# Turning the row maxima of a head group with VectorE's 32-wide transposes instead of TensorE's transpose and ScalarE's copy

## The reference

```python
xn = _layernorm(x, axis=-1)
x = x + _L0_attn_ref(xn, ...) + _L0_ffn_ref(xn, ...)
```

```python
attn = jnp.einsum('bhqd,bhkd->bhqk', q, k) * scale
attn = jax.nn.softmax(attn, axis=-1)
out = jnp.einsum('bhqk,bhkd->bhqd', attn, v)
```

## Time and profile before

| what | value |
|---|---|
| median of 3 runs | 946.4 us (944.36 to 946.92) |
| the profiled execution | 944.99 us, its span 943.2 us |
| granted TensorE clock over the span | 0.969 of full |
| PE busy | 871.3 us, 92% of the span |
| PEld busy | 605.1 us, 64% |
| DVE busy | 608.0 us, 64% |
| ACT busy | 583.3 us, 62% |
| POOL busy | 427.3 us, 45% |

### The profile page before, as it was taken

How to read it: one execution, slowest core, us unless ns; L and a number is a source line. 1 busy time by engine, 2 the same in 40 slices (tenths; PEclk the granted TensorE clock), 3 DMA queues, 4 the chain that set the end, 5 groups by cost and what they waited for, 6 DMA issues and landing times.

```text
span 943.2 us, 19555 instructions
## 1 busy us (share of the span) xinstructions
PE 871.3 (92%) x6491; PEld 605.1 (64%) x6492; DVE 608.0 (64%) x914; ACT 583.3 (62%) x941; POOL 427.3 (45%) x417
## 2 busy tenths in 40 slices
PE   5846999999999989889999999999999999999996
PEld 2436999999999976456556555555565465565462
DVE  6787844444444455676786786786777877776752
ACT  5855744444444442767767767767767866856764
POOL 2104722222222151753753764854754844744831
PEclk9965999999999999999999999999999999999997
DMA  9884555222222216554854755755755655654310
GB/s 315 315 265 149 187 151 172 72 72 68 76 67 69 65 47 171 157 154 101 203 158 118 198 159 127 198 155 130 189 163 130 192 161 130 191 141 109 76 48 23
DMA packets 91479, 133.74 MB, mean 142 GB/s; under 512 B 17512, under 2 KB 51824, under 8 KB 91024
## 3 DMA queue, kind: packets, MB, share of 16 engines
q1 hardware_dynamic: 84720, 114.95, 43.3%
q0 software_dynamic: 6480, 17.70, 7.1%
q10 hardware_dynamic: 208, 0.14, 0.0%
HBM read 76.10 MB, written 51.56 MB: 135 GB/s over the span
## 4 chain that ended last, share of the span: by engine, by line
PE 80%; DVE 11%; issue 3%; ACT 2%; DMA 2%; POOL 1%; DVEq 0%; ACTq 0%; POOLq 0%
PE bank L1463 12%; PE bank L1503 10%; PE s_pair L1412 9%; PE bank L1359 8%; PE s_pair L1341 8%; PE bank L1568 7%; PE st_pair L1491 6%; PE st_pair L1341 6%; DVE top L1934 4%; PE bank L1349 2%; PE bank L1324 2%; DMA xg<-xn_rows,token_of 1%; PE bank L1476 1%; PE bank L1517 1%; PE bank L1402 1%
## 5 line engine op out<-in xcount | busy, mean ns | idle before, releaser
L1934 DVE TENSOR_REDUCE top<-s_pair 128x2 f32<-128x1024 f32 x248 | 303.7, 1225 | 134.1 <-PE s_pair L1412 131.2
L1120 ACT ACTIVATE prob<-st_pair 128x1024 f32<-128x1024 f32 x252 | 259.1, 1028 | 116.9 <-PE st_pair L1491 109.1
L780 POOL DMA_INDIRECT xg<-xn_rows,token_of x71 | 82.7, 1165 | 207.5 <-PE bank L1324 157.3
L1463 PE MATMUL bank<-xT_b,w_sh 64*128 64x512 f32 x960 | 143.2, 404 | 0.5
L1412 PE MATMUL s_pair<-k_rows,q_rows 48*128 48x512 f32 x496 | 115.6, 459 | 12.0 <-DVE top L1934 11.8
L1503 PE MATMUL bank<-prob,v_ones 128*32 128x512 f32 x1024 | 124.8, 605 | 0.0
L1463 PEld LDWEIGHTS bank<-xT_b,w_sh 64*128 64x128 f32 x960 | 91.7, 187 | 31.1 <-issue 8.3
L1491 PE MATMUL st_pair<-q_rows,k_rows 50*128 50x512 f32 x504 | 106.2, 415 | 3.4 <-ACT prob L1120 2.6
L1359 PE MATMUL bank<-w_exp,c_hT 128*128 (+1 forms) x639 | 94.2, 292 | 0.6 <-ACT c_y L1027 0.6
L1412 PEld LDWEIGHTS s_pair<-k_rows,q_rows 48*128 48x128 f32 x496 | 47.4, 184 | 64.9 <-DVE top L1934 55.4
L1341 PE MATMUL s_pair<-w_exp,xg_T 128*128 x468 | 88.1, 338 | 0.0
(11 more groups left out here) (238 smaller groups left out, 1240.6 us busy)
## 6 DMA issues: line engine op xcount, KB each, us to landing
qk_rows<-qk_hi SPq DMA_DIRECT2D x56, 256.0 KB
q_rows<-qk_rows SPq DMA_DIRECT2D x64, 192.0 KB
k_rows<-qk_rows SPq DMA_DIRECT2D x56, 192.0 KB
expert_rows<-c_y SPq DMA_DIRECT2D x71, 128.0 KB, 1.7
qk_rows<-qk_lo SPq DMA_DIRECT2D x28, 256.0 KB
x_all<-in_L_attn_x_dram SPq DMA_DIRECT2D x8, 512.0 KB, 7.3
xn_rows<-x_n SPq DMA_DIRECT2D x8, 512.0 KB, 3.5
o_b<-in_L_attn_x_dram SPq DMA_DIRECT2D x8, 512.0 KB, 6.5
```

Of the source, the lines that this page charges most:

```text
L780: pool.indirect_dma_start(xg[s % 4][:, :], None, xn_dram, bass.IndirectOffsetOnAxis(token_of[:, s:s + 1], 0)).then_inc(c_x[s % 4], 16)
L1120: act.activation(prob[n % 3][:, 2 * jp:2 * jp + 2, :].rearrange("p j l -> p (j l)"), score_T_pair(b, g, t)[:, :], ACT.Exp, scale=HD ** -0. ...
L1463: ins = pe.matmul((g_bank, u_bank)[up][:, :], w_sh[rows, a, o:o + P], xT_of(b)[rows, c, k, :], start=(n == 0 and i == 0), stop=(n == 1 and ...
L1934: dve.tensor_reduce(top[g % 2][:, :, jp, qt], score_pair(b, g, v)[:, :].rearrange("p (i k) -> p i k", i=2), AX_X, ALU.max).then_inc(d_max, 1)
```

## The change

`turn_max` on PE and `max_rows` on ACT are gone. In their place `split_max` issues four more DVE instructions, each of which transposes 32 partitions x 32 columns of `top_parts` (the 16 columns and 16 beside them) into columns r to r + 31 of `top_T`; all four write partitions 0 to 31, and they read partitions from 0, 32, 64 and 96. `load_max` waits for them. PE's other uses of `m_bank`, which had waited for ACT's copy, now wait for what ran before it.

```diff
             def load_max(b, g):
-                wait(sp, a_mt, b * NG + g + 1)
+                wait(sp, d_mt, b * NG + g + 1)
...
-            def max_rows(b, g):
-                wait(act, b_mt, b * NG + g + 1)
-
-                wait(act, m_in[g % 2], (2 * b + g // 2) * 32)
-                act.activation(top_T[g % 2][:, :], m_bank[0:32, 0:P], ACT.Copy).then_inc(a_mt, 1)
...
-            def turn_max(b, g):
-                wait(pe, d_m, b * NG + g + 1)
...
-                pe.transpose(m_bank[0:32, 0:P], top_parts[g % 2][:, :, :, :, :].rearrange("p i a j t -> p (i a j t)").bitcast(F32),
-                             ident_f[:, :]).then_inc(b_mt, 1)
...
                 dve.tensor_tensor(dst[:, :, LO, :, :], src, dst[:, :, HI, :, :].bitcast(F32), ALU.subtract).then_inc(d_m, 1)
+                wait(dve, d_m, b * NG + g + 1)
+                wait(dve, m_in[g % 2], (2 * b + g // 2) * 32)
+                for r in range(0, P, 32):
+                    ins = dve.transpose(top_T[g % 2][:, r:r + 32], dst[r:r + 32, :, :, :, :].rearrange("p i a j t -> p (i a j t)").bitcast(F32))
+                ins.then_inc(d_mt, 1)
```

More of the change, by code:

```diff
@@ L261, in build_program @@
         top_parts = [sb(f"top_parts{i}", [P, 2, 2, 2, TPB], F32R, late) for i in range(2)]
-        top_T = [sb(f"top_T{i}", [32, P], F32R, late) for i in range(2)]
+        top_T = [sb(f"top_T{i}", [32, P], F32, late) for i in range(2)]
         xT_bs = [xT_b, xT_1]
@@ L343, in build_program @@
         inv_in = sem("inv_in")
[L345 to L351, removed]
+        b_r, b_v, b_qk, b_s, b_st, b_pv, b_gu, b_ha, b_res, b_dn, b_po = (
+            sem(f"b_{n}") for n in ("r", "v", "qk", "s", "st", "pv", "gu", "ha", "res", "dn", "po"))
+        a_r, a_v, a_qk, a_exp, a_th, a_uh, a_hh, a_ot, a_ao, a_res = (
+            sem(f"a_{n}") for n in ("r", "v", "qk", "exp", "th", "uh", "hh", "ot", "ao", "res"))
+        d_r, d_qk, d_max, d_mh, d_m, d_mt, d_ga, d_hb, d_inv, d_res, d_dn, d_po = (
+            sem(f"d_{n}") for n in ("r", "qk", "max", "mh", "m", "mt", "ga", "hb", "inv", "res", "dn", "po"))
         b_to, b_bo, d_to, a_bo, d_bo = (sem(n) for n in ("b_to", "b_bo", "d_to", "a_bo", "d_bo"))
@@ L655, in load_max @@
             def load_max(b, g):
-                wait(sp, a_mt, b * NG + g + 1)
+                wait(sp, d_mt, b * NG + g + 1)
                 for par in range(2):
                     sp.dma_start(q_rows[g][64 * par + 48:64 * par + 50, :, :].rearrange("a j (t q) -> a j t q", q=P).bitcast(F32),
-                                 top_T[g % 2][16 * par:16 * par + 16, :].bitcast(F32)).then_inc(m_in[g % 2], 16)
+                                 top_T[g % 2][16 * par:16 * par + 16, :]).then_inc(m_in[g % 2], 16)
             def move_sums(b, g):
@@ L1152, in slot @@
                         up_half(c, q)
-                    if t == 5 and there(nb):
-                        max_rows(nb, ng)
                     if now:
@@ L1181, in slot @@
                         last_o_high(0)
-            max_rows(0, 0)
             low_rank_high(1)
@@ L1396, in project @@
                 elif n == 1:
-                    wait(pe, a_mt, (b - 1) * NG + 2)
+                    wait(pe, d_qk, b * 4 + 1)
                 elif n == 2:
@@ L1400, in project @@
                 else:
-                    wait(pe, a_mt, (b - 1) * NG + 3)
+                    wait(pe, d_qk, b * 4 + 3)
                 pe.matmul(m_bank[:, :], w_rows[:, which, half * P:(half + 1) * P], r_rows[b % 2][:, which, :], start=True, stop=True).then_inc(b_qk, 1)
@@ L1510, in low_rank @@
                 wait(pe, xT_in, 16) if b == 1 else wait(pe, p_xl, b - 1)
-                if b <= 2:
-                    wait(pe, a_mt, 1 if b == 1 else 4)
+                if b == 1:
+                    pe.wait_ge(c_hed, NS - 1)
+                elif b == 2:
+                    wait(pe, d_qk, 8)
                 else:
@@ L1524, in project_values @@
                     wait(pe, r_in, b * 48 + 48)
-                    wait(pe, a_mt, b * NG + 1)
-                    if b == 0:
-                        pe.wait_ge(d_r, 2)
+                    wait(pe, d_r, b + 2) if there(b + 1) else wait(pe, d_po, (b - 1) * 2)
                 elif there(b + 1):
@@ L1530, in project_values @@
                 else:
-                    wait(pe, a_mt, b * NG + 2)
+                    wait(pe, a_v, b * 2 + 1)
                 for t in range(TPB):
@@ L1581, in project_o @@
                 elif h == 0:
-                    wait(pe, d_qk, (b + 2) * 4 + 4) if there(b + 2) else wait(pe, a_mt, (b + 1) * NG + 3)
+                    wait(pe, d_qk, (b + 2) * 4 + 4) if there(b + 2) else wait(pe, a_v, (b + 1) * 2 + 2)
                 else:
-                    wait(pe, a_mt, (b + 1) * NG + 4)
+                    wait(pe, d_po, b * 2 + 1)
                 for n in range(2):
@@ L1670, in slot @@
                         values(b, g, 1)
-                    if t == 4 and there(nb):
-                        turn_max(nb, ng)
                     if (g, t) == (1, 0) and now:
@@ L1693, in _ @@
             some_tiles(NS // RUN * RUN, last=True)
-            turn_max(0, 0)
             score(0, 1, 0)
@@ L1937, in split_max @@
                 wait(dve, d_max, b * 32 + g * 8 + 8)
-                wait(dve, b_mt, b * NG + g - 1)
+                wait(dve, d_mt, b * NG + g - 1)
                 dst = top_parts[g % 2]
```

## The result

The change takes 959.74 us in the median of four runs (956.57 to 962.18), the kernel before 946.66 in four runs beside it (944.36 to 948.04): a ratio of 1.014, 95% interval 1.0108 to 1.0172. The profiled executions are 956.57 and 944.99 us, 11.6 apart, so the profiles show nearly all of what the medians (13.1) do.

What follows compares the result with a forecast made beforehand. PE's queue plus its waits, chiefly for DVE's maximum, was taken to bound the kernel; delays beyond each group's room, net of PE's gains, sum to 14.3 us: 959.3 from the profiled 944.99, said as 960, range 949 to 967.

Steps and rivals of the forecast that it cites:

- The hold: DVE's four transposes, reading different groups of 32 partitions, and the step 3 operation do not overlap: 0.24 us a step.
- d: Delay of DVE at maximum 0, from the transposes ahead of the step 3 operation: 1.08 us.
- The wait behind the split, 0.21: On DVE, the first transpose starts 0.21 us after the subtract, the split's second half.
- The rooms, 0.62 in twelve and 0.91 in the g = 2 groups: Delay of maximum 0 that score 1 tolerates; beyond it, 0.46 us lost in each of twelve groups, 0.17 in six.
- The four in which PE waited already: Groups where score 1 already followed maximum 0 by 0.05 or 0.06 us: 1.08 us lost each, 4.3 together.
- the five between: Groups with rooms of 0.17, 0.32, 0.45, 0.50 and 0.50 us before score 1: 3.5 us lost together.
- The two near the end: Groups with room 0.68 us, where part of the delay falls in DVE's idle time: 0 lost.
- `add_down` late, 0.6 us: In six g = 2 slots, PE's down matmuls wait for a later `add_down`: 0.1 us each, 0.6 together.
- Full overlap: Rival: transposes overlap like ordinary small DVE operations, 0.11 us a step; 945 to 947 us, chance 0.12.
- faster rival: Rival: transposes some 0.05 us apart on DVE keep PE's 0.22; sum about -5, 940 to 941 us, chance 0.06.
- dear price: Rival: each DVE transpose as slow as a reciprocal, 0.38 us a step held; 975 us, chance 0.06.
- queue behind POOL: Rival: DVE transposes stopped by running POOL operations in four or five groups; 5 us more, 965 us, chance 0.16.

Runs made afterwards that it cites:

- added-alone run: Kernel before, keeping PE's transpose and ACT's copy, with DVE also making the four transposes into a tile nothing reads: 958.06 us, ratio 1.0156.
- first experiment: The change with all four DVE transposes reading partitions 0 to 31, instruction count unchanged: 944.15 us, ratio 0.9999 to the kernel before.

## Why the prediction was right

960 was forecast and 959.74 measured, inside the range. The mechanism held, but an agreement of 0.3 us is luck: the medians' difference has an interval of 10 to 16 us, and terms of the sum that were off balanced each other. The steps:

- **What bounds the kernel.** Held. PE has less to do and the kernel is slower; the wait that grew is the loop through `s_pair` (the earlier trace rows and its answer). The added-alone run shows the queue's gain turned into waiting.
- **The hold.** The step on which all hung was taken from a PSUM row for inputs in SBUF. The first experiment shows it: 0.213 from one transpose to the next against 0.107, 1.4% against nothing. Its size was somewhat off: 0.24 a step was forecast (0.21 and 0.03 behind it); the transposes last 0.199 and the next starts 0.014 after the end (0.84 us for four), so d is 1.00, not 1.08. The other bound, 0.19, was nearer. The Trainium skill states this hold in "VectorE: DVE Perf Modes", section "Two Vector instructions with no wait between them"; the runs agree for inputs in SBUF, 1.014 against 0.9999.
- **What is held.** Not everything behind them: in the five places without a step 3 operation, maximum 0, which reads PSUM alone, starts 0.98 us after the subtract, 0.06 before the last transpose ends; with the four behind the gate, maximum 1 starts at 512.26 and they end at 511.49 + 0.84 = 512.33. The step 3 operation, which also reads SBUF, waits for the end (512.40, next at 512.44). So the forecast that it is held was right, and it is not so for every follower.
- **The wait behind the split, 0.21.** Measured 0.20 (511.36 to 511.56). Held.
- **The rooms, 0.62 in twelve and 0.91 in the g = 2 groups.** 0.61 and 0.91 by the offsets. With d = 1.00 a typical group loses 0.38 where 0.46 was forecast, a g = 2 group 0.09 where it was 0.17. The same sum with d = 1.00 is 12 x 0.38 + 6 x 0.09 - 0.2 + 4 x 1.00 + (5.00 - 1.94) - 0.4 + 0.2 = 11.8 us against 11.6 between the profiles.
- **The sum, kind by kind.** Even this comes out in part by balance. By the offsets the twelve groups lost 6.6 us, not 4.6: eight lost 0.38 or 0.39, four lost 0.5 to 1.35, and in each of these a cast or subtract was stopped by POOL. The four in which PE waited already lost 2.5, not 4.0 (in one of them a cast was stopped before and is not now), the five between 3.5, not 3.1. The two near the end, put at 0, kept PE's gain: -0.22 each.
- **`add_down` late, 0.6 us.** The down matmuls do start later behind score 1 in a g = 2 slot, 0.66 us instead of 0.56 (568.00 - 567.34, below), but the next maximum is later by only 0.03. Mis-sized: 0.2 in all.

```profile
566.07 1.22 DVE L1906 TENSOR_REDUCE top<-s_pair 128x2 f32<-128x1024 f32 x1
567.20 0.75 DVE L1947 TENSOR_TENSOR o_b<-bank,o_b 128x256 f32<-128x256 f32 x2
567.34 0.50 PE L1403 MATMUL s_pair<-k_rows,q_rows 48*128 48x512 f32 x2 [0.24 <-DVE top L1906]
...
568.00 1.45 PE L1543 MATMUL bank<-w_sh,h_T 64*128 64x256 f32 x20
```

- **Score 1 at 0.05 after maximum 0.** In 27 of 31 groups (0.04 to 0.06). It was said for g = 0, 1 and 3; it holds in g = 2 as well, where 0.17 of loss was counted, so it could have been said of g = 2 too.
- **The wait of about 30 us.** 29.0.
- **The delays add up, none is made up.** Held: all maxima but 0 and 1 change the offset by 0.9 us together.
- **The rivals.** Full overlap is what the first experiment builds, and it costs nothing, as it was worked out (945 to 947 beside 946.4; measured 944.15 beside 944.5). The sum of the faster rival is about -4 us by its own terms, not -5; nothing hangs on it. The dear price is excluded by 199 ns. The queue behind POOL is excluded for the transposes: 28 of the 128 ran while a POOL `TENSOR_TENSOR` ran, and the longest of all took 203 ns. The cast and the subtract do get stopped, 12 of 64 times (6.9 us) after 11 of 64 (6.1 us) before, in other groups. That is much of the scatter in single groups, and it happens to balance here. The slot of the earlier trace rows has a cast stopped in place of a subtract:

```profile
473.23 1.29 POOL L818 TENSOR_TENSOR ao<-ao,o_sum 128x512 f32<-128x512 f32 x1
473.52 1.04 DVE L1913 CAST top_parts<-top 128x16 fp32r<-128x16 f32 x1
```

## What to carry to other kernels

Before work is moved off a full engine, look at what the receiving engine does in the loop that both meet in: measure its room ahead of the next thing that is waited for (here 0.62 us), and price the addition against that room, not against its idle share (DVE was a third idle, and the kernel lost 1.4%). A gain on one engine and a delay on the other in front of the same wait do not add; the later one alone counts. Several small DVE operations that read different groups of 32 partitions can cost more than as many on one group (0.84 us against 0.48 for four). And time saved in front is lost again if the result needs longer on its way (one transpose instead of four saved DVE 0.6 us a group, and its DMAs cost the kernel 9%).

## What the runs showed of the hardware

- Four 32x32 transposes on DVE that read the same 32 partitions start 0.135, 0.093 and 0.093 us apart (199 ns for the first, 157 for the others). If each reads another group, all take 199 ns and start 0.213 apart. One transpose of 128 x 32 takes 211 ns: four separate ones took 840.
- A maximum that reads PSUM from partition 0 was not held by a transpose of partitions 96 to 127 in SBUF: it began 0.06 us before that one ended.
- DVE's cast and subtract from SBUF were stopped by a running POOL `TENSOR_TENSOR` until its end (up to 1.28 us for 0.17). DVE's transposes (28 of 128 beside such an operation) and its operations that read PSUM never were.
- After PE stood still for 3.67 us the clock was granted at 0.50, and 16 matmuls took 3.64 us, not 1.92.
